# Image 0 in eight loads, full-height idle matmuls released by events, and an instruction order of their own for images 0 to 3, in a batched depthwise-convolution kernel

## What is computed

```python
def gn(v):                       # one group per channel: normalise each 128x128 plane
    m, s = mean(v), var(v)       # over the plane
    return (v - m) / sqrt(s + 1e-5)

v    = gn(x)
avg  = v.mean(axis=(2, 3))                        # (16, 32)
dyn  = avg @ w1.T + b1                            # (16, 288)
wk   = sigmoid(dyn).reshape(16 * 32, 1, 3, 3)     # a 3x3 filter for each plane
y    = depthwise_conv3x3(v, wk) + conv_bias
out  = x + (v - y) * fscale * v + y
```

## Time and profile before

| | |
|---|---|
| median of 3 runs | 306.94 us (306.54 to 307.16) |
| the profiled execution, its own time | 307.99 us |
| its span, first to last instruction | 306.2 us |
| PE busy | 283.8 us, 93% |
| DVE, ACT, POOL busy | 246.8, 200.8, 243.6 us |
| image 0's first convolution matmul | 24.67 us after the span's start |
| a middle image | 16.76 us |

### The profile page before, as it was taken

One profiled execution on the slowest core, in us unless ns is written; L12 is line 12 of the kernel. 1 busy time (PEld: TensorE's weight loads), 2 busy tenths in 40 slices (PEclk: granted clock), 3 DMA queues, 4 the chain that ended last, 5 costly groups with the idle time before them and its releaser, 6 DMA issues.

```text
span 306.2 us, 6427 instructions
## 1 busy us (share of the span) xinstructions
PE 283.8 (93%) x2276; PEld 252.4 (82%) x2276; DVE 246.8 (81%) x584; ACT 200.8 (66%) x338; POOL 243.6 (80%) x337
## 2 busy tenths in 40 slices
PE   0189979999999999999999999999999999999994
PEld 0148858979999898999999998989899999988883
DVE  3877696797989889898989898888989897646444
ACT  1156763866968686868769686868587696867600
POOL 1251759579998989898998989897989989897663
PEclk9999997999999999999999999999999999999998
DMA  7999203853959496785949494968769323133355
GB/s 280 407 421 423 110 2 154 321 249 137 374 248 374 185 358 272 275 354 199 427 150 396 178 367 183 364 256 308 321 211 412 161 104 149 79 154 162 148 223 222
DMA packets 10365, 77.46 MB, mean 253 GB/s; under 512 B 1275, under 2 KB 1502, under 8 KB 2654
## 3 DMA queue, kind: packets, MB, share of 16 engines
q1 hardware_dynamic: 10334, 77.06, 63.9%
HBM read 39.30 MB, written 37.75 MB: 252 GB/s over the span
## 4 chain that ended last, share of the span: by engine, by line
PE 85%; DVE 4%; POOL 3%; issue 3%; DMA 3%; ACT 0%; SPq 0%; POOLq 0%; ACTq 0%; DVEq 0%
PE conv_ps L415 28%; PE conv_ps L418 24%; PE conv_ps L411 18%; PE conv_ps L407 11%; DMA xs<-x 3%; POOL outs L797 2%; DVE outs L547 1%; DVE pieces L492 1%; PE dyn_ps L381 1%; DVE outs L557 1%; PE stat_ps L346 1%; POOL numbers L747 1%; PE stat_ps L351 1%; DVE taps L516 1%; PE stat_ps L336 0%
## 5 line engine op out<-in xcount | busy, mean ns | idle before, releaser
L415 PE MATMUL conv_ps<-xs,taps 64*128 64x320 f32 (+1 forms) x512 | 172.4, 416 | 0.0
L797 POOL TENSOR_TENSOR outs<-outs,linear 128x1152 f32<-128x1152 f32 x63 | 165.6, 2638 | 6.9 <-DVE outs L547 6.9
L411 PE MATMUL conv_ps<-xs,taps 64*128 64x320 f32 (+1 forms) x512 | 170.3, 412 | 0.5 <-DVE taps L523 0.5
L407 PE MATMUL conv_ps<-xs,taps 64*128 64x320 f32 (+1 forms) x512 | 167.1, 406 | 0.0
L418 PE MATMUL conv_ps<-xs,taps 64*128 64x320 f32 (+1 forms) x512 | 166.2, 404 | 0.0
L547 DVE SCALAR_TENSOR_TENSOR outs<-xs,beta,conv_ps 128x576 f32<-128x576 f32 x128 | 103.5, 808 | 47.6 <-PE conv_ps L418 47.4
L668 ACT ACTIVATE linear<-xs,offset,gain 128x576 f32<-128x576 f32 x128 | 109.1, 856 | 2.4 <-POOL outs L797 2.4
L492 DVE BATCH_NORM_STATS2 pieces<-xs 128x6 f32<-128x64 f32 (+1 forms) x256 | 102.2, 447 | 5.9 <-DMA xs<-x 5.9
L418 PEld LDWEIGHTS conv_ps<-xs,taps 64*128 64x128 f32 x512 | 96.1, 188 | 6.7
L407 PEld LDWEIGHTS conv_ps<-xs,taps 64*128 64x128 f32 x512 | 96.1, 188 | 1.8 <-issue 0.4
L646 ACT ACTIVATE xs<-xs,neg_mean 128x576 f32<-128x576 f32 x128 | 97.3, 763 | 0.0
(11 more groups left out here) (61 smaller groups left out, 182.6 us busy)
## 6 DMA issues: line engine op xcount, KB each, us to landing
xs<-x SPq DMA_DIRECT2D x30, 1188.0 KB, 10.4
out<-outs SPq DMA_DIRECT2D x30, 1152.0 KB, 5.2
xs<-x SPq DMA_DIRECT2D x4, 594.0 KB, 6.0
out<-outs SPq DMA_DIRECT2D x3, 576.0 KB, 2.8
out<-outs SPq DMA_DIRECT2D x2, 288.0 KB, 2.6
cst<-const SPq DMA_DIRECT2D x1, 248.0 KB, 7.7
w1s<-w1r SPq DMA_DIRECT2D x1, 111.4 KB
gates<-gate SPq DMA_DIRECT2D x1, 8.0 KB
```

Of the source, the lines that this page charges most:

```text
L407: nc.tensor.matmul(bank_of(i, g, h), pair(i, g, 0, 0), columns(i, g, h, 0, 1), start=False, stop=False).then_inc(even_done, 1)
L411: nc.tensor.matmul(bank_of(i, g, h), pair(i, g, 0, 2), columns(i, g, h, 0, 0), start=True, stop=False)
L415: nc.tensor.matmul(bank_of(i, g, h), pair(i, g, 1, 1), columns(i, g, h, 1, 0), start=False, stop=False)
L797: nc.gpsimd.tensor_tensor(tile, tile, linear[:, PAIR * k:PAIR * (k + 1)].rearrange("p g n -> p (g n)"), ALU.add).then_inc(out_ready, 1)
```

## The change

It does five things.

1. Image 0 is loaded in eight pieces (one group each) instead of four. The small tensor `gate` is loaded right after the first piece, and the constants are cut in two: the first 129 columns (`average` and `counts`, `STAT_COLS`) are loaded ahead of the last two pieces, the rest after them, then the weights. Each has its own semaphore, and each engine waits for the one that it needs.
2. For image 0, `count` is done on DVE (`count_first`) right before `rows`, and the copy of the band constants stands behind `rows(0)`.
3. `keep_warm` issues one matmul of all 128 rows, and each call waits for an event of another engine (a finished `bn`, a mean, a copied statistic and so on). Eleven of these replace the six.
4. On PE the chain products of the next image stand three banks later for images 1 to 4, and mean and spread three later for images 2 to 4; `spread` of images 2 to 4 is now ahead of banks 0 and 1 of the next image, instead of ahead of banks 12 and 13 (15 and 0 for image 2).
5. DVE, ACT and POOL get an order to match, for images 0 to 3 (`LATE = 3`). For image 5 `spread` stands at banks 14 and 15 instead of 12 and 13. From image 5 on the order of every engine is as before, but for `bn` and `matrices`, which change places ahead of product 5.

```diff
+LATE = 3
-FIRST_LOADS = 4
+FIRST_LOADS = 8
...
-            load_first()
-            sp.dma_start(cst[:], const).then_inc(consts_loaded, 16)
-            sp.dma_start(w1s[:], w1r).then_inc(params_loaded, 16)
-            sp.dma_start(gates[:].rearrange("p a g -> p (a g)"), gate).then_inc(params_loaded, 16)
+            load_first(0, 1)
+            sp.dma_start(gates[:].rearrange("p a g -> p (a g)"), gate).then_inc(gates_loaded, 16)
+            load_first(1, FIRST_LOADS - 2)
+            sp.dma_start(cst[:, 0:STAT_COLS], const[:, 0:STAT_COLS]).then_inc(stat_consts_loaded, 16)
+            load_first(FIRST_LOADS - 2, FIRST_LOADS)
+            sp.dma_start(cst[:, STAT_COLS:], const[:, STAT_COLS:]).then_inc(consts_loaded, 16)
+            sp.dma_start(w1s[:], w1r).then_inc(weights_loaded, 16)
...
-                    late = 3 if j <= 2 else 0
+                    late = 3 if i <= LATE else 0
...
-                if i == 1 and at == 0:
-                    spread_odd(2)
+                if 0 < i <= LATE:
+                    if at == 0:
+                        spread_even(i + 1)
+                    if at == 1:
+                        spread_odd(i + 1)
...
-                    late = 3 if j == 2 else 0
+                    late = 3 if i < LATE else 0
...
-                    if at == 12 + late:
+                    if at == (14 if i == LATE else 12) and not late:
                         spread_even(j)
-                    if at == 13 + late:
+                    if at == (15 if i == LATE else 13) and not late:
                         spread_odd(j)
...
+            def keep_warm(s, value, columns):
+                pe.wait_ge(s, value)
+                nc.tensor.matmul(conv_ps[:, CONV_TILES - 1, BANK:BANK + columns], const_of("average"),
+                                 cst[:, 0:columns], start=True, stop=True)
+
+            keep_warm(pieces_done, GROUPS - 1, STAT_COLS)
+            keep_warm(pieces_done, GROUPS, STAT_COLS)
             mean_whole(0)
+            keep_warm(neg_mean_ready, 1, STAT_COLS)
+            keep_warm(dev_ready, 1, STAT_COLS)
             spread_whole(0)
-            keep_warm(3)
+            pe.wait_ge(consts_loaded, 16)
+            keep_warm(zstats_copied, 1, WARM)
+            for k in range(3):
+                keep_warm(pieces_done, GROUPS + 3 + k, WARM)
             pe.wait_ge(last_columns_set, 1)
             averages(0)
-            pe.wait_ge(params_loaded, 32)
+            pe.wait_ge(weights_loaded, 16)
             dynamics_whole(0)
-            keep_warm(2)
+            keep_warm(dyn_done, 1, WARM)
+            keep_warm(own_dyn_ready, 1, WARM)
+            keep_warm(dyn_ready, 1, STAT_COLS)
             mean_whole(1)
-            keep_warm(1)
+            keep_warm(tap_ready, 1, STAT_COLS)
...
+            def count_first():
+                dve.wait_ge(stat_consts_loaded, 16)
+                dve.wait_ge(pieces_done, GROUPS)
+                nc.vector.tensor_scalar(pieces[:, 0, :, 1], pieces[:, 0, :, 1], const_of("counts"), None,
+                                        ALU.mult).then_inc(counted_ready, 1)
...
             for i in range(B):
+                if 0 < i <= LATE:
+                    deviation(i + 1)
+                    average_columns(i + 1)
+                    add_pair(i - 1, 3)
                 if nxt:
                     scales(i + 1)
                 add_pair(i, 0)
+                if i <= LATE:
+                    add_pair(i, 1)
+                    scaled_taps(i + 1)
+                    second_moments(i + 2)
+                    add_pair(i, 2)
...
```

More of the change, by code:

```diff
@@ L55 @@
 _N = 0
-for _name, _width in (("average", PARTS), ("band", HALF), ("centre", GROUPS * SETS),
-                      ("spread", INPUTS), ("phase", PARTS), ("own", SLOTS), ("counts", 1)):
+for _name, _width in (("average", PARTS), ("counts", 1), ("band", HALF), ("centre", GROUPS * SETS),
+                      ("spread", INPUTS), ("phase", PARTS), ("own", SLOTS)):
     _AT[_name] = (_N, _N + _width)
     _N += _width
+STAT_COLS = PARTS + 1
 CONST_COLS = _N
@@ L293, in load, with load_first @@
                                  x[i][:, per * h * LAID:per * (h + 1) * LAID]).then_inc(x_loaded[i % XBUFS][h], 16)
-            def load_first():
+            def load_first(first, last):
                 per = GROUPS // FIRST_LOADS
-                for k in range(FIRST_LOADS):
+                for k in range(first, last):
                     sp.dma_start(xs[:, 0, per * k:per * (k + 1)].rearrange("p g k w -> p (g k w)"),
@@ new lines, in _, with bn_next @@
+            order = [(j, g) for j in range(2, B) for g in range(GROUPS)]
+            done = [0]
+            def bn_next(count):
+                for j, g in order[done[0]:done[0] + count]:
+                    bn(j, g)
+                done[0] += count
+            bn_next(START_AHEAD)
+            share = {0: (1, 1, 1, 1, 0, 0, 1, 1), 1: (2, 2, 1, 1, 0, 1, 1, 1), 2: (2, 2, 1, 1, 0, 1, 1, 1),
+                     3: (2, 1, 2, 1, 0, 1, 1, 1), 4: (1, 2, 1, 1, 1, 1, 1, 1)}
+            for i in range(B):
+                nxt, stats, late = i + 1 < B, i + 2 < B, i < LATE
+                for g in range(GROUPS):
+                    if stats and g == 4 and late:
+                        rows(i + 2)
+                    bn_next(share.get(i, (1,) * GROUPS)[g])
+                    if stats and g == 2 and not late:
+                        rows(i + 2)
+                    if nxt and g == 5:
+                        matrices(i + 1)
+                    if i == B - 1 and g == GROUPS - 1:
+                        add_last(GROUPS - 2)
+                    product(i, g)
+                    if nxt and g == 2 + (i <= LATE):
+                        own_taps(i + 1)
@@ L683, in _ @@
             copy_averages(0)
+            count(1)
             centre(0, 3)
-            centre(0, 4)
             sigmoid(0)
-            count(1)
-            for g in range(5, GROUPS):
+            for g in range(4, GROUPS):
                 centre(0, g)
@@ L802, in _ @@
             average_columns(0)
+            pool.wait_ge(inv_ready, 1)
             scales(0)
@@ L812, in _ @@
                 add_pair(i, 0)
[L813 removed]
+                if i <= LATE:
+                    add_pair(i, 1)
                     scaled_taps(i + 1)
[L815 removed]
                     second_moments(i + 2)
[L817 to L830 removed]
+                    add_pair(i, 2)
+                    if i == LATE:
+                        deviation(i + 2)
+                        average_columns(i + 2)
+                        add_pair(i, 3)
+                else:
+                    if nxt:
+                        scaled_taps(i + 1)
+                    if stats:
+                        second_moments(i + 2)
+                    add_pair(i, 1)
+                    if stats:
+                        deviation(i + 2)
+                        average_columns(i + 2)
+                    add_pair(i, 2)
+                    if i < B - 1:
+                        add_pair(i, 3)
 def kernel(x, L0_conv_w1, L0_conv_b1, L0_conv_fscale, L0_conv_conv_bias):
```

108 lines of the change are left out of this document (16 added, 92 removed).

## The result

The changed kernel takes **307.97 us** (median of 13 runs, 307.58 to 310.18), the kernel before 307.31 beside it: ratio **1.0037** (95% 1.0021 to 1.0053), where 0.98 was forecast. It is slightly slower, by 0.4%. The profiled execution has a time of 310.07 and a span of 308.2; ten of the 13 lie between 307.6 and 308.1.

What follows compares the result with a forecast made beforehand. It took PE, busy 93% of the span, to bound the kernel from image 3 on. 307.99 - 2.8 - 4.28 + 1.65 + 0.65 - 0.85 = 302.4, with the median 1.05 lower at 301.3 us; range 298.0 to 304.3.

Steps and rivals of the forecast that it cites:

- the start: Up to the first convolution and its low clock: earlier loads and count gain 2.8 us, bounds 1.1 to 5.0.
- the hand-over in images 3 and 4: Image 3's late second_moments(5) and image 4's late start on POOL: 0.4 + 0.25 = 0.65 us lost.
- rival D: Image 0's loads: small pieces load slower; at half rate image 0 comes 6.2 us later, 307.5; chance 0.03.
- The clock: Around the first convolution: full-height idle matmuls may raise the clock early; 1.0 us of loss after the first bank assumed.
- The wait for the moments: Image 0, ahead of bank 1: PE waits 1.2 us at spread_even(1) if the start is early.
- rival A: The clock stays low at the start, so 1.7 us more, 303.0; chance 0.17.
- The fall: The low clock at 47.36, after PE's 2.07 us wait, goes away: 1.72 us gained.
- Rival C: The clock's fall at 47.36 has another cause than the wait and stays: 1.72 more, 303.0; chance 0.04.
- The waits: PE's waits for second_moments(2) at 45.93 and matrices(2) at 66.74 go: 2.07 and 0.49 us gained.
- Rows late: Images 0 to 2: own_taps ahead of rows on DVE makes PE wait 0.55 us, three times, 1.65 lost.
- POOL's list: POOL in images 1 to 3: 12.3 us of steps, taps done at 14.2, fits by 0.6 us, nothing charged.
- E: POOL late in images 1 to 3, PE waiting for matrices at each start: 11.4 us more, 312.7; chance 0.04.

Runs made afterwards that it cites:

- i2: The kernel before, unchanged, run again for another profile; 306.7 us.
- f3: The changed kernel, unchanged, run again for a second profile; 308.74 us.
- e4: The changed kernel with, in image 3, image 4's averages copied before image 5's count and image 5's deviation and average columns before the third pair; 305.76 us.
- f1: The kernel of e4 with all constants, weights and gates behind the eight loads of image 0; 303.4 us.
- g1: The kernel of f1 with the spread of image 1 at banks 3 and 4 of image 0 instead of 1 and 2; 303.26 us.
- h1: g4 with image 5's moments ahead of image 3's second pair, image 1's negative mean two tiles earlier, gates ahead of the other constants; 300.46 us.
- g4: The kernel of f1 with the mean a bank later and, on POOL in images 0 to 3, scaled taps ahead of the second pair; 303.9 us.

## Why the prediction was wrong

i2 and f3 are profiles of the two kernels in which the clock rises once, behind the first convolution, and stays. Their spans are 304.9 and 306.9, and the 2.0 between them divides so (minus is gained; the parts are rounded):

| part | forecast | i2 to f3 | how |
|---|---|---|---|
| start and low clock | -2.8 | +0.5 | first convolution 24.05 to 25.64; low for 7.90 to 5.66, half of it lost |
| rest of image 0 | -2.07 + 0.55 | -1.9 | length 23.46 to 20.45, less the 1.1 counted above |
| images 1, 2 | -0.49 - 1.72 + 1.1 | -0.1 | 17.99 + 16.95 to 17.44 + 17.44; i2 has no fall that could go |
| images 3, 4 | +0.65 | +3.8 | 16.76 twice to 18.54 + 18.75 |
| rest | -0.85 (the unnamed) | -0.2 | image 10, 17.04 to 16.80 |

Two steps of the prediction failed, each by over 3 us: the start, forecast to gain 2.8 where it lost 0.5, and the hand-over in images 3 and 4, forecast to lose 0.65 where it lost 3.8.

- **The start** (forecast 2.8, bounds 1.1 to 5.0) failed at two sentences. The first priced gates and constants at 0.2 + 0.1 us; the second said of image 1 that "the change does not bring forward" its landing. It never asked whether the change puts it back. It does, by 1.36 (by 1.67 from i2 to f3), and the three idle matmuls that wait for its `bn` are ahead of `averages(0)`: 19.93 instead of 17.8 to 18.2. I had named that queue, and taken the wrong time for its head. Eighths gained nothing, since the last `bn` instruction of image 0 begins at 11.00 (10.73 before). This is rival D's mechanism at a fraction of its price, and in part by another cause: the two small loads among the eighths, which no rival had. The mean, forecast at 12.0, came at 12.91.
- **The clock.** That full height raises it before the convolution holds in four profiles of ten, and 1.0 us of low clock was a fair size for those: behind the first bank e4 and f1 have one low stretch of 3.41 us each, 1.7 lost, and g1 and h1 none. The wait for the moments, forecast at 1.2, is 0.76 in e4 and f1. In the other six it is rival A.
- **The fall** (1.72) was read from one profile as a fixed cost. It comes in a part of the executions, at about 0.8 us each. Rival C, another cause, isn't borne out: in no profile without the wait is there a fall in that place.
- **The waits** of 2.07 and 0.49: gone, as forecast.
- **Rows late**: forecast 0.55 for each of images 0 to 2, measured 0.74 to 0.88 at bank 10. Images 1 and 2 take 17.44 where 17.3 was forecast. Right in mechanism.
- **POOL's list**: "fits by 0.6 us, the thinnest place". Its steps were summed rightly: the tap of image 2 is done 14.1 us after image 1's start (forecast 14.2). But the list closes on itself: the `add_pair` that opens it waits for the last product of the image before, and that stands behind `matrices` and so behind the tap. (In the changed kernel it waits 1.94 us for that product, until 64.16.) The taps of images 1, 2 and 3 begin at 43.68, 61.19 and 78.70 there, 17.51 apart, where an image takes 17.44, so nothing is to spare. To take away the mean's wait alone brought nothing, both limits together 1.4 for images 1 and 2; POOL's alone wasn't tried.
- **Images 3 and 4** (forecast 0.65, measured 3.8). For the hand-over I followed one step, `second_moments(5)`, and took the rest as covered; that step is borne out by the 0.8 that e4 leaves. Two other steps, `copy_averages(4)` behind `count(5)` and `average_columns(5)` behind an `add_pair`, stood in the order of the change to be read. Neither of them was in a rival; my slower case, E, looked for POOL at the start of images 1 to 3.
- **The chances**: "all but D, E and F" is 0.91, not 0.92.

## What to carry to other kernels

Where two orders of work meet, follow every queue through the one or two rounds of the hand-over: the wait stands in front of what was moved least, and 3 us were mended here by two moves. A new order of loads in a full queue can put back all that is behind it even where the bytes ahead stay the same, as they do here for image 1; name who waits for the load behind. An idle matmul queued ahead of real work on another engine's event takes over that event's lateness. A term of the clock read from one profile (here the fall, 1.72) needs a second profile before it is priced.

## What the runs showed of the hardware

- With all DMA engines busy (share 0.96 to 1.06 from 3 to 10 us) the load queue moved 392 to 409 GB/s in quarters, 355 to 388 in eighths, and 313 to 334 in eighths with a load of 64-byte rows and one of 516-byte rows among them.
- Idle matmuls of 128 rows brought the high clock (2.4 GHz) before the convolution in some profiles and not in others of the same start. Those of 64 rows, at the same places, did so in none of three profiles. The Trainium skill (TensorE: Matmul & The Clock Gate, Part 1) says that the point of the rise differs from run to run of one kernel, and the trace agrees (29.59 to 31.95 in four profiles of the kernel before, 18.86 in f1 and 31.2 in g4 with the same start); it says nothing of rows.
- A wait of PE of 2.06 to 2.07 us in the same place was followed by a fall to 1.2 GHz in three profiles and by none in the fourth.
